# Neighbour stage of a graph layer: indirect transfers that add into the node rows, in place of gather, buffer and addition

## What is computed

```python
edge_index = jnp.stack([src, dst])
# graph layer; xn = layernorm(x)
agg = jnp.zeros_like(xn).at[edge_index[0]].set(xn[edge_index[1]])   # one neighbour per node, the last one wins
x = x + jnp.concatenate((xn, agg), axis=-1) @ W.T + b
# mixture of 8 experts, 2 of them for each node; t = layernorm(x)
probs = softmax(t @ router_w.T); rw, re = top_k(probs, 2); rw = rw / rw.sum(-1)
out = t
for e in range(8):
    y = gelu(t @ w1[e] + b1[e]) @ w2[e] + b2[e]
    out = out + combine[:, e:e+1] * y
x = x + out
```

## Time and profile before

| | us |
|---|---|
| median of 3 runs (lowest, highest) | 1187.66 (1182.05, 1188.21) |
| span of the profiled execution, first to last instruction | 1180.7 |
| neighbour stage in it, first gather to the end of the last `route` | 452.6 to 643.9 |

### The profile page before, as it was taken

The page is one execution under the profiler, slowest core; times in us unless marked ns, Lnnn a source line. Parts: engine busy times, 40 slices in busy tenths (PEclk is TensorE's granted clock), DMA queues, the critical chain, the costliest instruction groups (busy, mean ns, idle before and its releaser), DMA issues.

```text
span 1180.7 us, 28647 instructions
## 1 busy us (share of the span) xinstructions
PE 836.3 (71%) x9319; PEld 702.9 (60%) x9319; DVE 868.3 (74%) x1893; ACT 630.4 (53%) x1669; POOL 484.9 (41%) x527
## 2 busy tenths in 40 slices
PE   1599888887666862243444468888888888888886
PEld 1588887776555651132333256776766666767766
DVE  6999999995677764477688946776667666766666
ACT  3466666663444331264553345666666565666665
POOL 7000000004445556764650035555555555555554
PEclk9799999999888795555555789999999999999999
DMA  8800000003664444553551712222222222222220
GB/s 228 266 28 27 27 27 27 27 27 84 208 202 149 118 121 144 156 165 99 160 170 63 7 42 68 64 65 61 65 66 64 64 65 66 63 67 65 70 60 11
DMA packets 79211, 104.89 MB, mean 89 GB/s; under 512 B 22593, under 2 KB 64538, under 8 KB 78994
## 3 DMA queue, kind: packets, MB, share of 16 engines
q0 software_dynamic: 21408, 54.87, 16.6%
q1 hardware_dynamic: 57714, 48.76, 14.8%
HBM read 63.16 MB, written 44.01 MB: 91 GB/s over the span
## 4 chain that ended last, share of the span: by engine, by line
PE 31%; DVE 28%; issue 14%; another core or an unknown queue 12%; ACT 8%; DMA 3%; POOL 1%; ACTq 1%; DVEq 1%; SPq 1%; POOLq 0%
PE bank L983 12%; PE bank L997 9%; DVE arena L1099 7%; PE bank L786 6%; DVE arena L1082 5%; ACT arena L750 2%; PE bank L951 2%; PE bank L809 1%; ACT arena L711 1%; DVE bst L1300 1%; DVE arena L1283 1%; DVE big L1297 1%; POOL arena L517 1%; ACT arena L695 1%
## 5 line engine op out<-in xcount | busy, mean ns | idle before, releaser
L983 PE MATMUL bank<-arena,w1s 128*128 128x128 f16 x3000 | 211.2, 220 | 78.0 <-issue 69.1
L983 PEld LDWEIGHTS bank<-arena,w1s 128*128 x3000 | 177.8, 98 | 112.8 <-issue 109.8
L505 POOL DMA_INDIRECT arena<-key_rows,cid x98 | 94.8, 968 | 330.0 <-DVEq L1215 252.7
L750 ACT ACTIVATE arena<-bank,b1s 128x128 f32<-128x128 f32 x500 | 142.0, 368 | 155.6 <-remote 152.1
L532 POOL DMA_INDIRECT out<-arena,gidx x125 | 140.3, 1123 | 188.9 <-DVE arena L1438 149.5
L997 PE MATMUL bank<-w2s,arena 128*128 x1500 | 184.1, 272 | 1.4 <-DVE arena L1418 0.7
L521 POOL DMA_INDIRECT arena<-tok_rows,gidx x125 | 124.4, 995 | 107.4 <-DVE gidx L1407 69.4
L809 PE MATMUL bank<-wgs,arena 128*128 128x256 f16 x1176 | 160.0, 289 | 5.6 <-issue 5.4
L1433 DVE SCALAR_TENSOR_TENSOR arena<-bank,arena 128x256 f32<-128x256 f32 x125 | 60.1, 481 | 132.7 <-remote 129.5
L997 PEld LDWEIGHTS bank<-w2s,arena 128*128 128x128 f16 x1500 | 140.7, 98 | 17.8 <-issue 1.7
L809 PEld LDWEIGHTS bank<-wgs,arena 128*128 128x128 f16 x1176 | 121.7, 104 | 34.1 <-issue 8.6
(11 more groups left out here) (215 smaller groups left out, 1414.9 us busy)
## 6 DMA issues: line engine op xcount, KB each, us to landing
agg_rows<-arena SPq DMA_DIRECT2D x49, 256.0 KB
tok_rows<-arena SPq DMA_DIRECT2D x13, 896.0 KB
big<-x SPq DMA_DIRECT2D x5, 1792.0 KB, 14.1
arena<-w SPq DMA_DIRECT2D x16, 256.0 KB, 2.9
big<-x SPq DMA_DIRECT2D x6, 512.0 KB
arena<-tok_rows,gidx POOLq DMA_INDIRECT x125
out<-arena,gidx POOLq DMA_INDIRECT x125
arena<-key_rows,cid POOLq DMA_INDIRECT x98
```

Of the source, the lines that this page charges most:

```text
L505: gp.indirect_dma_start(er[:, b % 2, s, :], None, key_rows, bass.IndirectOffsetOnAxis(cid[:, t:t + 1], 0)).then_inc(er_full[b % 2], 16)
L750: last = sc.activation(h32[:, u % 2, at:at + P], bank[2 + u % 2][:, at:at + P], ACT.Gelu, bias=b1s[:, ds(e[x], 1), f], scale=1.0 / SCALE)
L983: last = mm(bank[2 + u % 2][:, at:at + P], parts[x, w, c, f], a[:, u % 4, c * P:(c + 1) * P], start=(n == 0), stop=(n == 5))
```

## The change

The gather of line 517 becomes an indirect transfer with `compute_op=ALU.add` whose destination is `xs[:, t, :]`: the DMA engines read the neighbour's row and the node's row and write the sum into the node's row. The buffers `pg`, their semaphores `pg_full` and `pg_used`, GpSimd's wait for `pg_used` and VectorE's 15 additions of line 1297 go. VectorE waits for the piece's own semaphore `summed[n]` and begins with `bn_stats`. GpSimd waits once, ahead of the first gather, until all tiles have had their own product added (`self_taken`, `self_added`), where VectorE waited for `self_added` before. The place in SBUF that `pg` had stays empty. `ROUTED` is 28, 28, 20 and 22 tiles, and the third `route` stands after piece 11 and not after piece 12.

```diff
--- before.py
+++ after.py
@@ -45,16 +45,12 @@
 TBANK = [0, 1, 4, 5]
 PBANK = [4, 5, 0, 1, 6, 7]
 RG = 28
-ROUTED = [(n, min(RG, T - n)) for n in range(0, T, RG)]
+ROUTED = [(0, 28), (28, 28), (56, 20), (76, 22)]
 PIECES = [(n, B) for n in range(0, T - B, B)] + [(91, 4), (95, 3)]
 TURNED = [(n, t, min(2, first + more - t)) for n, (first, more) in enumerate(PIECES) for t in range(first, first + more, 2)]
 OB = 7
 SCALE = 64.0
 EPS = 1e-5
-
-
-def gathered(n):
-    return 16 * sum(PIECES[k][1] for k in range(n % 2, n + 1, 2))
 
 
 def turned(t):
@@ -197,13 +193,14 @@
 
         two = Arena(arena, arena_bytes)
         t32 = Arena(arena, arena_bytes).take([P, 2, B, D], f32)
+        t32_end = 2 * B * D * SIZE[f32]
         er = two.take([P, 2, B, 2 * CH], i32)
         found = two.take([P, B, CH], f32)
         wm = two.take([P, B], f32)
         wmi = two.take([P, B], i32)
         wabs = two.take([P, B], f32)
 
-        pg = two.take([P, 2, B, D], f32)
+        two.at += t32_end
         tTh = two.take([P, 4, 2 * D], f16)
         tTl = two.take([P, 4, 2 * D], f16)
         rwx = two.take([P, 2, E], f32)
@@ -276,8 +273,7 @@
         er_used, gat_ready = sem("er_used"), sem("gat_ready")
         consts3_ready = sem("consts3_ready")
         s_b2, b2_scaled = sem("s_b2"), sem("b2_scaled")
-        pg_full = [sem("pg_full0"), sem("pg_full1")]
-        pg_used = sem("pg_used")
+        summed = [sem(f"summed{n}") for n in range(len(PIECES))]
         t_ready, tt_ready, ttc_ready, lg_ready = sem("t_ready"), sem("tt_ready"), sem("ttc_ready"), sem("lg_ready")
         ttl_ready, rw_ready = sem("ttl_ready"), sem("rw_ready")
         rows_stored = [sem("rows_stored0"), sem("rows_stored1")]
@@ -508,14 +504,13 @@
             pool.wait_ge(agg_stored[0], 16 * (T // 4 + 1))
             pool.wait_ge(agg_stored[1], 16 * (T // 4))
             pool.wait_ge(s_brow, 16)
+            pool.wait_ge(self_taken, IB)
+            pool.wait_ge(self_added, T // 2 - IB)
             for n, (first, more) in enumerate(PIECES):
                 pool.wait_ge(gat_ready, (first + more - 1) // B + 1)
-                if n >= 2:
-                    pool.wait_ge(pg_used, n - 1)
-                for s in range(more):
-                    t = first + s
-                    gp.indirect_dma_start(pg[:, n % 2, s, :], None, agg_rows,
-                                          bass.IndirectOffsetOnAxis(gat[:, t:t + 1], 0)).then_inc(pg_full[n % 2], 16)
+                for t in range(first, first + more):
+                    gp.indirect_dma_start(xs[:, t, :], None, agg_rows, bass.IndirectOffsetOnAxis(gat[:, t:t + 1], 0),
+                                          compute_op=ALU.add).then_inc(summed[n], 16)
 
             def gather_tile(j):
                 gp.indirect_dma_start(xg[:, j % DEPTH, :], None, tok_rows,
@@ -876,7 +871,8 @@
                 pe.wait_ge(ttl_ready, m + 1)
                 for h in range(more):
                     t = first + h
-                    to = bank[LBANK[t // RG]][:, t % RG * E:(t % RG + 1) * E]
+                    c = max(n for n, (at, _) in enumerate(ROUTED) if at <= t)
+                    to = bank[LBANK[c]][:, (t - ROUTED[c][0]) * E:(t - ROUTED[c][0] + 1) * E]
                     k = 0
                     for c in range(2):
                         for a, w in ((tTh, 0), (tTh, 1), (tTl, 0)):
@@ -885,7 +881,7 @@
                             k += 1
                 last.then_inc(lg_ready, 1)
 
-            early = turned(3 * RG)
+            early = turned(ROUTED[3][0])
             for m in range(4):
                 turn(m)
             for m in range(4, early):
@@ -1290,12 +1286,9 @@
             step(ve.tensor_copy(rwh[:, 0, :, :].rearrange("p c e -> p (c e)"), rwx.rearrange("p c e -> p (c e)")))
             ve.tensor_tensor(rwh[:, 1, :, :], rwx, rwh[:, 0, :, :], ALU.subtract).then_inc(rw_ready, 1)
 
-            dve.wait_ge(self_added, T // 2 - IB)
             for n, (first, more) in enumerate(PIECES):
                 of = slice(first, first + more)
-                dve.wait_ge(pg_full[n % 2], gathered(n))
-                step(ve.tensor_tensor(xs[:, of, :], xs[:, of, :], pg[:, n % 2, 0:more, :], ALU.add))
-                dve.sem_inc(pg_used, 1)
+                dve.wait_ge(summed[n], 16 * more)
                 for s in range(more):
                     last = ve.bn_stats(bst3[:, s, :], xs[:, first + s, :])
                 step(last)
@@ -1311,7 +1304,7 @@
                                         ).then_inc(ln_ready, 1)
                 if n == 5 or n == 9:
                     route(n // 4 - 1)
-                if n == len(PIECES) - 3:
+                if n == len(PIECES) - 4:
                     low_turned(turned(first))
                     route(2)
 
```

## The result

The changed kernel took 1192.0 us against 1182.1 us (medians of 13 runs each), 1.009 times as long, interval 1.006 to 1.012. The forecast was 1211 us, 23 us above the 1187.7 us it started from: on the right side, and more than twice as far as the 9.9 us measured. Its profiled execution has a span of 1190.3 us against 1180.7.

A forecast was written before the change was run, and what follows sets the result against it. TensorE slows in unbroken transfer runs until GpSimd pauses. Stage end: 582 + 51.4 + 15.0 + 19.1 = 667.5 us against 643.9, so 1187.7 + 23.6 = 1211 us; own range 1198 to 1232, 8-in-10 range 1143 to 1245.

The forecast's parts named there:

- What bounds the kernel: Neighbour stage: unbroken indirect transfers slow TensorE after some 60 to 120 matmuls until GpSimd pauses; two buffers force pauses.
- The transfers add: GpSimd's step per adding transfer: 1.34 us, taken between the gather's 1.25 and the scatter's 1.42.
- The upper bound of 2.2: GpSimd's longest step per adding transfer, from twice the descriptors' time: 2 x 0.95 + 0.30 = 2.2 us.
- Rival B: Adding transfers are dear: at 2.2 us each the run lasts until 668 us; chance 0.13.
- its milder case: The dear-transfer rival with TensorE keeping up: stage ends at 683 us, +39, 1227 us.
- The brake goes: GpSimd issues 98 transfers without a wait, to 583.9 us; TensorE stays slow from about 482 to 586 us.
- TensorE's pace in the stretch: TensorE during the unbroken run: 1.63 matmuls/us, from the two slow stretches in the profile.
- The additions go: VectorE's neighbour additions removed: a piece takes 6.42 us instead of 7.83, 1.41 gained of 2.02.
- From there: After about 582 us: pieces 4 to 12 take 51.4 us, three `route` 15.0, the end 19.1.
- The third route: Moving the third `route` a batch forward costs or gains nothing; if transfers were the bound, it fills idle time.
- The wait for `self_added`: GpSimd's new wait ahead of the first gather costs nothing; the last store to `agg_rows` releases that gather.

The follow-up runs named there:

- g0: Changed kernel on chip 10 with plain transfers writing in place, neighbour addition left out: 1237.2 us, 1.038 times the kernel before.
- g4: Changed kernel on chip 10 with half-row transfers, pieces adding and writing in turn: 1169.6 us, one execution.
- h1: Changed kernel on chip 9 with plain transfers in place and a GpSimd memset behind each: 1203.5 us, 1.010 times the kernel before.
- e4: Kernel before on chip 6 with VectorE's additions left out, buffers and waits kept: 982.4 us, 0.983 times the kernel before.
- e2: Kernel before on chip 6 with 12 already met waits behind each gather, which took no time: 1001.1 us, ratio 1.001.
- e3: Changed kernel on chip 6 with the routing as before: 1040.7 us, 1.040 times the kernel before.
- f3: Kernel before on chip 4 with the routing alone changed: 996.6 us, 0.998 times the kernel before.
- e1: Changed kernel on chip 6 with transfers writing in place, nothing added: 980.3 us, 0.982 times the kernel before.
- f1: Changed kernel as it is, on chip 4: 1032.5 us, 1.033 times the kernel before.
- h3: Mixed version on chip 9: 3 of 7 tiles add in the transfer, VectorE adds the others tile by tile: 1170.4 us, 0.983 times the kernel before.
- g1: Changed kernel on chip 10 with only even tiles adding, odd ones written in place: 1171.7 us, 0.982 times the kernel before.

## Why the prediction was wrong

**What bounds the kernel** was read rightly. That an unbroken run at 1.25 us slows TensorE until 2 us after its end was the boldest reading, and g0 shows it within 3 us at either end.

**The transfers add**: this term failed. I took a step of 1.34 us, between the gather and the scatter, and the measured one is 1.84. The upper bound of 2.2 held it, and no row of before shows such a transfer. The scatter, 18% above the gather, was the wrong neighbour. Rival B was said to decide from 1.85 us on; by its own sum it does so from 1.80, where 452.6 + 98 x 1.80 + 15 = 644 us. At the measured step that sum is 452.6 + 98 x 1.84 + 15 = 648 us; the stage ended at 651.8, the rest being the late landing (6.90 us against 2.75). So B was right, with TensorE in good order as in its milder case, at 1.84 us instead of the 2.2 it was priced at. I had given it 0.13. The forecast's side came out right by luck: it was to come from slow stretches, and the changed kernel has none.

Stretches with hardly anything but transfers moving, of the changed kernel and of g0, then an adding and a plain one of g4's half rows:

```profile
460.00:468.00 8.00, 0.00 (x0) 0.00 (x0) 0.34 (x2) 0.00 (x0) 6.60 (x5) 0.50 0.50 66
```

```profile
500.00:510.00 10.00, 0.50 (x3) 0.42 (x4) 0.00 (x0) 0.00 (x0) 7.56 (x9) 0.50 0.36 105
```

```profile
461.00:467.00 6.00, 0.00 (x0) 0.00 (x0) 0.00 (x0) 0.00 (x0) 4.78 (x4) 0.50 0.28 33
...
472.00:477.00 5.00, 2.21 (x10) 1.44 (x10) 1.52 (x11) 3.25 (x7) 3.78 (x5) 0.50 0.20 52
```

An adding transfer takes the DMA engines 0.50 x 1.84 = 0.92 us, a plain one 0.36 x 1.25 = 0.45. By the Trainium skill's rule ("Collectives: The Full Stack", section "The bandwidth ceiling: the fold count and why AG ≠ RS ≠ AR") an add inside a transfer needs a second source read and so halves the rate (it says so of a reduce-scatter), and this trace agrees: twice as long. Half rows give the same factor, 0.28 x 1.84 = 0.51 us against 0.20 x 1.25 = 0.25, with half the bytes. It didn't set the time, since GpSimd was the bound.

**The brake goes**: right for plain transfers, wrong for these. The longer step that lengthens the run also leaves TensorE at speed; I had let the two terms vary by themselves, and between these two steps they exclude each other. That it is the pace, and not the kind of transfer, is shown for plain ones spaced evenly (h1) and argued for the adding ones. A step of 1.25 us costs slow stretches, one of 1.84 costs 58 us of run.

**TensorE's pace in the stretch**, 1.63 matmuls a us, was taken from short stretches, and is 36 / 95.7 = 0.38 in the long one. This term failed too, though the changed kernel does not show it. Had the step been 1.25 us, the forecast would have been +16 and the truth (g0 on chip 10, without any addition) +46.

**The additions go**: 13 x 1.41 = 18 us was forecast, 18.4 measured (e4). The number agrees in part by luck. The reason given was VectorE's loop; in e2 most additions wait for data, and with the additions 13 long transfers went, which shortens GpSimd's run from 137.1 to 122.6 us (e2, e4), 14.5 of the 18.4 us. In the changed kernel none of this shows, since VectorE waits for data.

**From there**: 6.42 us a piece was forecast, 6.56 measured in g0; `route` 5.3 and measured 11.53 - 6.56 = 4.97, the third 4.4 and measured 5.6; from `nmr` of piece 12 to the end 19.1, measured 697.3 - 677.0 = 20.3.

**The third route** fills idle time where the transfers are the bound, as said: 3.7 us (e3). Where they are not, it was to be worth nothing, and is worth 2.5 us in the kernel before (f3). **The wait for `self_added`** cost nothing: the first transfer starts at 452.62 us, 452.56 before.

**The sum as it came out**, from the lengths of the stage: writing in place, without additions and buffers and with the new routing, takes it from 164.9 to 145.5 us (e2, e1): -19.4. Adding in the transfer takes it to 199.0 (f1): +53.5, together +34 on chips like 4 and 6. On the others the kernel before loses 191.3 - 164.9 = 26.4 us more, the changed one nothing: +8.

## What to carry over

Before a copy is replaced by one that adds on its way, measure what the issuing engine pays for one: here 0.59 us more, whatever the bytes, and a run of such transfers then sets the stage. A wait that seems to waste an engine's time may keep another engine going, so look at what stops, and when, each time it is lifted. And what a change is worth can depend on the chip: the same change costs 0.5 to 0.9% on one kind of chip here and 3.3% on another.

## What was not expected of the hardware

- Chips of two kinds: the kernel before takes 999 to 1001 us on two chips and 1182 to 1194 on four measurements of others, with TensorE idle for "issue" 69.1 us against 4.3 in the last stage alone.
- On the slower kind evenly spaced plain indirect transfers slow TensorE at 1.25 and 1.44 us a step, and not at 1.70; mixed with adding ones at a mean step of 1.35 us, and at 1.53 and 1.58 only by a few single gaps (12.7 us in h3, 20.3 in g1).
- An adding indirect transfer takes GpSimd 1.54 us instead of 0.95, for whole rows and half rows alike. Plain ones take 0.95 us with 32 packets and with 16.
- VectorE's addition of 1792 elements a partition in one instruction makes the indirect transfer beside it 1.6 to 2.8 us long instead of 0.95, in either form tried. Cut into instructions of 256 elements, it leaves the transfer at 0.95.
